# One TensorE-bound kernel, the same work issued in another order on every engine

## What is computed

```python
# first layer, per batch; C = 64 in the reference, a whole batch at once in the kernel
v     = x @ W_write.T
S     = r @ w.T                      # w is x shifted by one row
reads = (S * decay_mask) @ v         # plus the state of earlier chunks
x1    = layernorm(x + (x + alpha * reads @ W_read.T))
# second layer
gate  = q(x1) @ q(w_gate).T          # q: FP4 quantise and dequantise in blocks of 16
y     = q(x1) @ q(w_up).T            # 704 columns each
h     = silu(gate) * y
out   = layernorm(x1 + q(h) @ q(w_down).T)
```

## Time and profile before

| quantity | value |
|---|---|
| median of 3 runs | 320.72 us |
| the profiled execution's own time | 319.53 us |
| its span, first to last instruction | 317.8 us |
| PE busy | 299.8 us (94%) |
| DVE busy | 278.9 us (88%) |
| POOL busy | 241.5 us (76%) |
| ACT busy | 223.8 us (70%) |
| mean granted clock of TensorE | 0.982 |

### The profile page before, as it was taken

One profiled execution on the slowest core, in us unless ns is written; L12 is line 12 of the kernel. 1 busy time (PEld: TensorE's weight loads), 2 busy tenths in 40 slices (PEclk: granted clock), 3 DMA queues, 4 the chain that ended last, 5 costly groups with the idle time before them and its releaser, 6 DMA issues.

```text
span 317.8 us, 6470 instructions
## 1 busy us (share of the span) xinstructions
PE 299.8 (94%) x1911; PEld 271.1 (85%) x1911; DVE 278.9 (88%) x725; ACT 223.8 (70%) x545; POOL 241.5 (76%) x258
## 2 busy tenths in 40 slices
PE   6949999999999989999999999999999999999783
PEld 2939988999899879889999998999999998899682
DVE  4996699969999999999988996989998899998953
ACT  7582986679677488669785886686877758587563
POOL 2897886476968967896978889487998757769671
PEclk9996999999999999999999999999999999999979
DMA  6704011832637446433562269338463273267601
GB/s 223 279 35 134 1 68 34 140 74 86 185 75 121 92 86 144 157 95 98 150 180 75 65 107 198 88 104 151 103 120 84 67 112 84 71 136 130 77 33 66
DMA packets 38722, 34.36 MB, mean 108 GB/s; under 512 B 25760, under 2 KB 31776, under 8 KB 38688
## 3 DMA queue, kind: packets, MB, share of 16 engines
q1 hardware_dynamic: 32064, 22.81, 34.5%
q10 hardware_dynamic: 6624, 11.15, 11.1%
HBM read 22.87 MB, written 5.18 MB: 88 GB/s over the span
## 4 chain that ended last, share of the span: by engine, by line
PE 67%; POOL 9%; issue 7%; DVE 7%; DMA 6%; ACT 3%; SPq 1%; ACTq 0%; POOLq 0%; DVEq 0%
PE ps L2160 15%; PE ps L2161 15%; PE ps L2164 15%; PE ps L2173 5%; PE ps L2174 5%; PE ps L2170 5%; DMA h_gT<-h_g 4%; POOL h_q L504 3%; DMA w_pair<-in_w_attn_dram 2%; PE ps L2224 2%; POOL h_n L485 1%; DVE hqT_lo L1584 1%; PE ps L2269 1%; POOL pr_lo L445 1%; PE ps L2283 1%
## 5 line engine op out<-in xcount | busy, mean ns | idle before, releaser
L2160 PE MATMUL ps<-guT_hi,xqT_hi 128*128 128x512 f32 (+1 forms) x192 | 74.0, 385 | 1.5 <-ACT xqT_hi L822 1.4
L2161 PE MATMUL ps<-guT_lo,xqT_hi 128*128 128x512 f32 (+1 forms) x192 | 72.1, 375 | 0.0
L504 POOL TENSOR_TENSOR h_q<-h_gT,h_sT 128x768 f32<-128x768 bf16 x30 | 51.8, 1731 | 12.3 <-DVE hqT_lo L1584 10.7
L2164 PE MATMUL ps<-guT_hi,xqT_lo 128*128 128x512 f32 (+1 forms) x192 | 56.5, 375 | 0.0
L485 POOL TENSOR_TENSOR h_n<-w_raw,h_rs 128x704 f32<-128x704 f32 x32 | 47.1, 1473 | 9.0 <-DVE h_rs L1414 8.9
L2160 PEld LDWEIGHTS ps<-guT_hi,xqT_hi 128*128 128x128 f32 x192 | 36.1, 188 | 6.8 <-ACT xqT_hi L822 1.7
L445 POOL TENSOR_TENSOR pr_lo<-pr,pr_hi 128x512 fp32r<-128x512 f32 (+3 forms) x32 | 28.5, 901 | 16.8 <-ACT pr_hi L791 16.8
L2164 PEld LDWEIGHTS ps<-guT_hi,xqT_lo 128*128 128x128 f32 x192 | 35.5, 188 | 6.0 <-DVE xqT_lo L1521 0.2
L2161 PEld LDWEIGHTS ps<-guT_lo,xqT_hi 128*128 128x128 f32 x192 | 36.1, 188 | 4.5
L2160 PE MATMUL ps<-dnT_hi,hqT_hi 128*128 128x256 f32 x160 | 39.6, 283 | 0.0
L2161 PE MATMUL ps<-dnT_lo,hqT_hi 128*128 128x256 f32 x160 | 39.5, 283 | 0.0
(11 more groups left out here) (130 smaller groups left out, 852.1 us busy)
## 6 DMA issues: line engine op xcount, KB each, us to landing
h_sT<-h_scales_dram SPq DMA_DIRECT2D x30, 384.0 KB
out_dram<-wq_gu ACTq DMA_DIRECT2D x31, 128.0 KB, 1.8
xs<-in_x_rows_dram ACTq DMA_DIRECT2D x7, 512.0 KB, 4.6
x_full<-in_xt_rows_dram ACTq DMA_DIRECT2D x6, 512.0 KB, 3.7
w_raw<-in_w_ffn_dram SPq DMA_DIRECT2D x6, 352.0 KB, 6.0
h_scales_dram<-h_s SPq DMA_DIRECT2D x30, 32.0 KB, 2.6
w_pair<-in_w_attn_dram SPq DMA_DIRECT2D x1, 512.0 KB, 5.1
x_full<-in_xt_rows_dram SPq DMA_DIRECT2D x1, 512.0 KB, 3.5
```

Of the source, the lines that this page charges most:

```text
L504: nc.gpsimd.tensor_tensor(h_q[:, p, :], h_gT[:, p, :, :].rearrange("p c t -> p (c t)"), h_sT[:, p, :], ALU.mult).then_inc(h_quant, 1)
L2160: nc.tensor.matmul(dst, lh, rh, start=(first and i == 0), stop=False)
L2161: nc.tensor.matmul(dst, lh, rl, start=False, stop=False)
L2164: last = nc.tensor.matmul(dst, ll, rh, start=False, stop=(end and i == len(terms) - 1))
```

## The change

The same calls stand in another order on PE, DVE, ACT, POOL and SP, with the same helpers and the same number of calls on each engine. The tables of PSUM banks and the bank waits that follow from them are other numbers. Data, tile sizes, transfers and helpers are the same. Of the tables and of the lists, the diff at the places that matter here:

```diff
-        s_at = ((6, 3, 3, 4),
-                (4, 7, 5, 3),
+        s_at = ((6, 3, 5, 4),
+                (4, 3, 1, 7),
...
@@ PE, start @@
             reads(0, 0, [(v_lo_ready, 1)])
             scores(0, 3, [(w_grid, 1)])
-            w_transpose(0, [(z_ready, 1)])
+            w_transpose(0, [(v_lo_ready, 2)])
             w_transpose(1, [(comb_lo_ready, 1)])
+            values(1, 0, [(pr_ready, 3)])
             w_subtract(0)
             w_subtract(1)
-            reads(0, 1, [(w_grid, 2)])
-            scores(1, 0, [(w_grid, 3)])
...
+            scores(1, 0, [(pr_ready, 4)])
+            scores(1, 1, [(wT_lo_ready, 1)])
+            reads(0, 1, [(w_grid, 3)])
...
@@ PE, end @@
             down(29, 1, [(h_grid, 32)])
-            down(30, 2, [(hT_lo_ready, 62)])
-            h_transpose(31, 3, 0, [(o_ready, 30)])
-            h_transpose(31, 3, 1, [(o_ready, 29)])
-            down(31, 3, [(o_ready, 31)])
+            h_transpose(31, 3, 0, [(o_ready, 29)])
+            h_transpose(31, 3, 1, [(hT_lo_ready, 62)])
+            down(30, 2, [(hT_lo_ready, 61)])
+            down(31, 3, [(hT_lo_ready, 64)])
...
@@ POOL, start @@
             x_rest(1, 0)
+            x_rest(1, 1)
+            x_stats(0, 0)
             w_normalise(2)
-            x_stats(0, 0)
             w_normalise(3)
             p_rest(0, 2)
             p_rest(0, 3)
-            x_rest(1, 1)
+            x_normalise(0, 0)
...
@@ POOL, end @@
+            h_spread(27, 1, 14)
             out_stats(24, 0)
-            h_spread(27, 1, 14)
             h_spread(28, 0, 15)
             h_normalise(30, 0)
             out_stats(25, 1)
+            h_spread(29, 1, 15)
             h_normalise(31, 1)
-            h_spread(29, 1, 15)
             h_dequant(30, 0)
```

More of the change, by code:

```diff
@@ L593, in _ @@
             p_rest(3, 3)
             h_normalise(9, 1)
-            x_rest(4, 0)
-            x_rest(4, 1)
+            h_spread(6, 0, 4)
+            out_stats(2, 0)
             x_normalise(3, 0)
+            p_rest(4, 0)
+            p_rest(4, 1)
+            x_stats(3, 1)
+            x_dequant(3, 0)
+            out_stats(3, 1)
+            h_normalise(10, 0)
+            p_rest(4, 2)
+            x_normalise(3, 1)
             h_spread(7, 1, 4)
-            x_dequant(3, 0)
-            h_normalise(10, 0)
@@ L631, in _ @@
-            h_spread(13, 1, 7)
-            h_normalise(15, 1)
+            h_normalise(12, 0)
+            h_spread(10, 0, 6)
+            x_stats(4, 1)
+            h_normalise(13, 1)
+            h_spread(11, 1, 6)
+            p_rest(5, 0)
+            out_stats(8, 0)
+            x_normalise(4, 1)
+            h_spread(12, 0, 7)
+            h_normalise(14, 0)
+            x_dequant(4, 1)
+            out_stats(9, 1)
+            h_spread(13, 1, 7)
+            out_stats(10, 0)
+            h_normalise(15, 1)
@@ L633, in _ @@
+            h_spread(14, 0, 8)
+            h_normalise(16, 0)
+            p_rest(5, 1)
+            p_rest(5, 2)
+            p_rest(5, 3)
+            h_normalise(17, 1)
+            x_rest(6, 0)
+            x_rest(6, 1)
             x_stats(5, 0)
-            out_stats(8, 0)
-            out_stats(9, 1)
-            h_spread(14, 0, 8)
+            out_stats(11, 1)
+            h_spread(15, 1, 8)
+            x_stats(5, 1)
             x_normalise(5, 0)
-            out_stats(10, 0)
-            h_normalise(16, 0)
@@ L670, in _ @@
             x_rest(7, 0)
[L671 to L679 removed]
+            x_rest(7, 1)
+            h_normalise(18, 0)
+            x_dequant(5, 1)
+            x_stats(6, 0)
+            x_stats(6, 1)
+            h_spread(16, 0, 9)
+            h_normalise(19, 1)
+            x_normalise(6, 0)
@@ new lines, in _ @@
+            out_stats(12, 0)
+            h_spread(17, 1, 9)
+            x_dequant(6, 0)
+            x_normalise(6, 1)
+            out_stats(13, 1)
+            h_spread(18, 0, 10)
+            h_normalise(20, 0)
+            h_spread(19, 1, 10)
+            h_normalise(21, 1)
+            out_stats(14, 0)
+            out_stats(15, 1)
+            x_dequant(6, 1)
+            h_normalise(22, 0)
+            out_stats(16, 0)
+            p_rest(7, 0)
+            h_spread(20, 0, 11)
+            p_rest(7, 1)
@@ L680, in _ @@
+            h_normalise(23, 1)
+            out_stats(17, 1)
+            x_stats(7, 0)
+            h_spread(21, 1, 11)
             out_stats(18, 0)
+            x_normalise(7, 0)
+            h_normalise(24, 0)
             h_spread(22, 0, 12)
-            p_rest(7, 1)
-            x_dequant(6, 1)
+            x_dequant(7, 0)
+            out_stats(19, 1)
+            h_spread(23, 1, 12)
             p_rest(7, 2)
-            h_normalise(23, 1)
-            out_stats(19, 1)
-            x_stats(7, 0)
```

1907 lines of the change are left out of this document (927 added, 980 removed).

## The result

The changed kernel took 317.55 us, the median of 20 runs (313.59 to 321.43), against 320.40 us for 20 runs of the kernel before (318.56 to 323.29). The ratio is 0.990, 95% interval 0.987 to 0.992: faster by about 1.0%. The profiled execution took 317.73 us with a span of 316.0 us, 1.8 us less than the span of before.

A forecast was written before the change was run, and what follows sets the result against it. PE was taken as the bound between 38.3 and 299.5 us (259.03 of 261.2 us busy), losing time at both ends. 319.53 - 3.4 + 1.4 - 0.8 = 316.7 us, forecast left at 316.5 us, range 311.5 to 322.5.

The forecast's parts named there:

- faster: Whole kernel: a time below 317.5 us, 1% of the median being what a measurement can tell; chance 0.52.
- term 2: Long middle: DVE's margin shrinks and new waits take some of PE's lead; +1.4 us, bounds -2.2 and +6.9.
- term 3: End: longer wait for h_dequant(30), no wait before the last down, a likely shorter transpose landing; -0.8 us, bounds -4 and +2.
- Term 1: Start: work fills PE's waits and the clock doesn't fall; -7.2 + 2.6 + 1.2 = -3.4 us, bounds 0 and -4.9.
- margin of 3.0 us: Up to gate_up(6): PE's work from the start 68.5 us against DVE's 65.5; margin down from 10.0 us.
- The 4.8 us: Start: what PE still loses there, so that it gets to gate_up(6) at about 73.3 us.
- The wait for L494: End: PE's wait for h_dequant(30), 3.4 us before, forecast to be 3 to 4.5 us.
- new bank waits: Priced within the middle's +1.4 us; each bank's last reader mostly an instruction that DVE did well before.
- the whole lead kept: Rival: no wait for weights, none new in the middle, transpose landing in about 5 us; 312.0 us, chance 0.15.
- DVE taking all: Rival: the start's waits come back before tile 9 and only the end changes; 319.1 us, chance 0.25.
- Contention: Rival: denser order makes DVE and POOL stretch each other, 6.8 us on PE's path; 323.5 us, chance 0.03.

The follow-up runs named there:

- experiment 1: Changed order up to 35 us, the order of the kernel before behind it; 322.64 us, ratio 1.006 to the kernel before.
- experiment 6: Kernel of experiment 1 with gate_silu(0) put before x_squares(0, 1) on ACT and hidden(0) before x_magic_add(0, 1) on DVE; 319.58 us, ratio 0.998.
- experiment 11: Changed kernel with x_squares(0, 1) before gate_silu(0) on ACT, x_magic_add(0, 1) and x_to_grid(0, 1) before hidden(0) on DVE; 320.62 us, ratio 0.999.
- experiment 12: Kernel of experiment 10 plus a one-column Silu in ACT's idle time at 8 us, moving the table load there; 313.81 us, ratio 0.977.
- experiment 2: Changed order up to 276 us, the end of the kernel before behind it; 317.49 us, ratio 0.990.
- experiment 7: Changed kernel with h_normalise(31) put back in front of h_spread(29) on POOL; 317.72 us, ratio 0.992.
- experiment 4: Changed kernel with matmuls on zeros added, 7 before down(28) and 13 before h_transpose(30); 317.67 us, ratio 0.990.
- experiment 10: Kernel of experiment 7 with other end banks, h_rest_all(28) before h_magic_add(30), matmuls on zeros (13 for 10 at start, 8 before h_transpose(30)); 315.21 us, ratio 0.985.
- experiment 3: Changed kernel with down(28) in PSUM bank 3 in place of bank 7; 319.43 us, ratio 0.992.

## Why the prediction was right, and where it was not

The time, 316.5 us forecast and 317.55 measured, and the sign were right, the sign by little: the gain of 1.0% is the line that the forecast drew for "faster". The closeness of the time is luck in part. In the profiled executions the terms came out at -3.4, -0.3 and +2.0 us where -3.4, +1.4 and -0.8 were put; term 2 was 1.7 us too dear and term 3 2.8 us too cheap, and most of it cancelled.

**Term 1, -3.4 us: right, with its mechanism.** Forecast: first `gate_up` at about 34.8 us with `reads(1, 0)` done and the clock at 1.00 over 23 to 30 us. Seen: 35.85 us, done, 1.00. PE came 3.4 us ahead. (The 34.8 us don't follow from the term: with `reads(1, 0)` done, 38.23 + 1.06 - 3.4 is 35.9.) The first `gate_up` waited 0.7 us for the last weight remainder (L763), where 1.2 was put; the row at 38.23 of the earlier trace rows, cited for that wait, shows none in the kernel before. All waits from 17 to 38.3 us came to 2.9 us (21.30 - 18.36) instead of 3.8. That the sum still met 3.4 has to do with 0.3 us by which the first L2300 came later (7.55 against 7.21 us); the rest wasn't traced. No run took the start's own edits apart.

**Term 2, +1.4 us: the step that failed.** Put at +1.4, it measured -0.3: the lead grew by 0.3 us between the first `gate_up` and `down(27)`. The step counted the work ahead of `gate_up(6)` on DVE and PE, found a margin of 3.0 us left and priced new waits for DVE. (The 4.8 us that it takes PE to lose at the start are nowhere added up; term 1 has 2.6 + 1.2 = 3.8.) There was none: in the stretch from 38.3 to 73.3 us DVE was 94% busy (32.75 of 35.0 us) and PE waited for it not once. From the first `gate_up` to 289.5 us PE stood idle 1.3 us in all, not 3 to 4:

```profile
35.85:289.50 253.65, 252.34 (x1613) 230.03 (x1613) 234.59 (x604) 184.62 (x465) 199.30 (x208) 1.00 0.51 108
```

That idle time is one wait, for ACT, an engine that the step's count left out, at 41.21 us; the old wait of 1.4 us for `xq_round` is gone. A count of work tells whether an engine can keep up on average; it says nothing on which call stands in front of which. Experiments 1, 6, 11 and 12 show that the sequence there is what matters: the places of `gate_silu(0)` and `hidden(0)` are worth 2 to 3 us when put first and 3 us, the whole gain, when put last. The 1.4 us was the price of a mechanism that did not act, and the one that could have made the forecast fail outright, with a price of 3 us, was named in no rival.

**Term 3, -0.8 us: mis-sized, its sign not shown.** In the profiled executions the end lost 2.0 us behind `down(27)`; exchanged whole (experiment 2) it costs 1.3 us by the trace, and 0 within about 1.6 us by the medians. Its parts: the 0.79 us wait before the last `down` is gone, as forecast. `h_normalise(31)` between `h_spread(29)` and `h_dequant(30)` was put at 1.39 us, +0.7 net; undone, it gave nothing (experiment 7), because bank 6 waited next. The wait for L494 was 2.7 us, under the 3 to 4.5 forecast, with 1.8 us waited one step earlier, for a bank. The forecast had put the new bank waits inside term 2, each bank's last reader being "mostly an instruction that DVE did well before"; that was wrong at two places of the end, L1424 both times, the second seen once the first wait was shorter (experiment 7).

**The rivals.** Up to 291 us the trace is nearest to the whole lead kept (0.15), though with a lead of 3.4 us and not 4.9; the case against it, the margin of 3.0 us on DVE, was the weak argument. DVE taking all (0.25) did not happen (its sum takes 0.4 us for the end where term 3 has 0.8); experiment 11 shows that ACT could have done it. Contention didn't grow: the thirty `h_rest_all` averaged 1056 ns in the changed kernel and 1118 ns before.

**What stays open.** Whether the changed end costs time at all: 1.3 us by the traces, none by the medians. How much of the profiled end's loss is landing and how much clock: single runs of the changed kernel reach from 313.6 to 321.4 us, with a mean clock of 1.00 at 313.59 us, 0.989 at 316.83 and 0.980 at 317.73. Why filling alone (experiment 4) shortened the end by 2 us in its trace and not the median. Of experiment 10's edits only the sum is shown.

## What to carry to other kernels

When a reordering makes the bounding engine arrive earlier, list for each of its first waits the exact call that frees it, and what stands in front of that call in its own queue, waiting for somebody else: here the place of two such calls decided the whole 1%. Count work to see who can keep up, but read queues to see who will. A wait removed from a chain of hidden waits may show nothing: take them away together, and move table loads into idle time before the first call that needs them. Compare two traces between the same two places of the work: a start that took 1.2 us more hid the shorter end of experiment 4.

## What the runs showed of the hardware

The clock of TensorE fell behind single waits of 2.98 and 3.64 us at the start of the middle (mean 0.95 over the 35 us from 38.3) and stayed at 1.00 behind one of 1.25 us. Matmuls on zeros kept it at 1.00 through the end, where the changed kernel had 0.50 for five microseconds. The eight matmuls of L2300, behind a wait of 1.1 to 2.1 us for a transfer, took 1.97 us in nine traces and 3.1 to 3.8 us in five; in three of the five (experiments 1 to 3) the granted clock between 7 and 11 us was 0.59 to 0.63, where the nine had 1.00. `h_rest_all`, a DVE operation with two SBUF inputs, took 0.95 us alone and 1.7 to 2.4 us where POOL's `h_spread`, `h_normalise` or `h_dequant` ran beside it for most of its time, and POOL's `h_normalise` 2.11 us instead of 1.39 where it began beside one. In the kernel of experiment 7:

```profile
290.61 2.11 POOL L485 TENSOR_TENSOR h_n<-w_raw,h_rs 128x704 f32<-128x704 f32 x1
...
295.84 1.66 POOL L504 TENSOR_TENSOR h_q<-h_gT,h_sT 128x768 f32<-128x768 bf16 x1 [0.64 <-issue]
```

```profile
289.57 1.90 DVE L1584 TENSOR_TENSOR hqT_lo<-h_q,hqT_hi 128x768 fp32r<-128x768 f32 x1 [0.36 <-ACT hqT_hi L871]
...
296.01 2.30 DVE L1584 TENSOR_TENSOR hqT_lo<-h_q,hqT_hi 128x768 fp32r<-128x768 f32 x1
```
